# Differential attention: spread query split on GpSimd, query rows on ScalarE, earlier row transposes on TensorE

## The reference, cut to what matters

```
h  = layernorm(x)                          # rows of 256
q, k = rotary(h @ Wq, h @ Wk); v = h @ Wv  # 16 heads, 2 sets of probabilities
p_r = softmax(q_r k_r^T * scale + causal)  # r = 0, 1
a  = p_0 v - lambda * p_1 v                # per head, then RMS norm over its 16 values
x  = x + (a * gain * (1 - lambda_init)) @ Wo
```

## Time and profile before

| | |
|---|---|
| median of 3 runs | 1345.92 us (1343.61 to 1348.31) |
| the profiled execution | 1350.3 us, span 1348.3 us |
| mean granted TensorE clock | 0.964 |
| granted clock from 134.8 to 168.5 us (fifth of the page's 40 slices) | 0.7 of full speed |
| busy share of the span | PE 91%, DVE 71%, ACT 52%, POOL 34% |
| differential attention | from 0 to about 227 us of the span |

### The profile page before, as it was taken

One profiled execution on the slowest core, in us unless ns is written; L12 is line 12 of the kernel. 1 busy time (PEld: TensorE's weight loads), 2 busy tenths in 40 slices (PEclk: granted clock), 3 DMA queues, 4 the chain that ended last, 5 costly groups with the idle time before them and its releaser, 6 DMA issues. The chain is left out here.

```text
span 1348.3 us, 27677 instructions
## 1 busy us (share of the span) xinstructions
PE 1223.6 (91%) x9976; PEld 974.3 (72%) x9976; DVE 961.7 (71%) x1865; ACT 707.6 (52%) x1471; POOL 454.6 (34%) x537
## 2 busy tenths in 40 slices
PE   5998797889898788699799999999997899999998
PEld 3676565344444367698677887878787899999998
DVE  6888686788888375788477777878675658555555
ACT  3777473678787536200356566565653463333332
POOL 2443542255544314466443242323321211112210
PEclk8999799799999978899899999999999999999999
DMA  5111052033232030000400000000000300000001
GB/s 172 37 33 35 24 122 69 11 88 85 81 90 65 10 104 1 0 0 0 146 5 8 4 6 5 4 8 4 8 0 1 95 25 25 25 25 24 1 1 63
DMA packets 58657, 51.00 MB, mean 38 GB/s; under 512 B 9064, under 2 KB 50888, under 8 KB 58184
## 3 DMA queue, kind: packets, MB, share of 16 engines
q1 hardware_dynamic: 58574, 49.88, 13.2%
HBM read 37.93 MB, written 11.53 MB: 37 GB/s over the span
## 5 line engine op out<-in xcount | busy, mean ns | idle before, releaser
L839 DVE TENSOR_REDUCE fa_neg_max<-psum 128x2 f32<-128x512 f32 x256 | 163.5, 685 | 35.1 <-PE psum L1012 34.2
L898 ACT ACTIVATE fa_probs<-psum 128x1024 f32<-128x1024 f32 x128 | 130.4, 1020 | 45.6 <-PE psum L1017 44.7
L1869 PE MATMUL psum<-mo_xT_high,mo_w_high 128*128 128x256 f32 x512 | 144.5, 282 | 2.1 <-DVE mo_xT_low L2703 1.9
L1869 PE MATMUL psum<-mo_xT_low,mo_w_high 128*128 128x256 f32 x512 | 144.1, 282 | 0.0
L1869 PE MATMUL psum<-mo_xT_high,mo_w_low 128*128 128x256 f32 x512 | 143.5, 280 | 0.0
L2535 ACT ACTIVATE mo_silu<-psum 128x256 f32<-128x256 f32 x128 | 49.1, 385 | 154.7 <-PE psum L1869 154.7
L2669 DVE TENSOR_TENSOR mo_mid<-mo_silu,psum 128x256 f32<-128x256 f32 x128 | 53.6, 420 | 92.8 <-ACT mo_silu L2535 92.7
L1012 PE MATMUL psum<-stacks_k_stack,stacks_q_stack 48*128 48x256 bf16 x512 | 93.0, 286 | 17.0 <-DVE fa_neg_max L839 8.5
L2005 POOL TENSOR_TENSOR ga_probs<-ga_probs,ga_top 128x1024 f32<-128x1024 f32 x16 | 30.5, 1906 | 205.4 <-DVE ga_top L2159 205.4
L1869 PEld LDWEIGHTS psum<-mo_xT_high,mo_w_high 128*128 128x128 f32 x512 | 96.3, 188 | 2.5 <-DVE mo_xT_low L2703 2.1
L1869 PEld LDWEIGHTS psum<-mo_xT_low,mo_w_high 128*128 128x128 f32 x512 | 96.4, 188 | 0.0
(11 more groups left out here) (433 smaller groups left out, 3575.7 us busy)
## 6 DMA issues: line engine op xcount, KB each, us to landing
k_parts<-da_k_parts SPq DMA_DIRECT2D x96, 64.0 KB, 2.0
stacks_k_stack<-k_parts SPq DMA_DIRECT2D x32, 192.0 KB
q_parts<-stacks_parts SPq DMA_DIRECT2D x48, 64.0 KB, 2.0
stacks_q_stack<-q_parts SPq DMA_DIRECT2D x32, 96.0 KB
x<-in_x SPq DMA_DIRECT2D x4, 512.0 KB, 5.8
da_context<-in_ctx SPq DMA_DIRECT2D x4, 512.0 KB, 7.6
stacks_q_stack<-q_parts SPq DMA_DIRECT2D x32, 64.0 KB
fa_context<-in_ctx SPq DMA_DIRECT2D x16, 128.0 KB, 2.2
```

Source lines behind the costliest of these rows:

```text
L839: nc.vector.tensor_reduce(neg_max[:, b, :, head_at(h)], ps[:, h % 2, :].rearrange("p (q k) -> p q k", q=2), AX.X, ALU.max, negate=True).th ...
L898: nc.scalar.activation(probs[:, g].rearrange("p h k q -> p h (k q)"), ps[:, 2 + 2 * (g % 2):4 + 2 * (g % 2), :], ACT.Exp).then_inc(exp_don ...
L1869: done = nc.tensor.matmul(out, lhsT[i], rhs[j], start=start and k == 0, stop=stop and k == 2)
```

## The change

`NORM_TURN` becomes 5. The statistics of the four tiles are taken at the end of turn 5. ACT takes the reciprocal root at the start of turn 6, behind the squares. DVE scales it at the end of turn 6 and makes one more small array, `q_offset` = -mean x rstd. ACT then makes one tile of `q_rows` and its high part in each of turns 7 to 10, in front of the copies of the turned probabilities. POOL splits one tile of queries in each of turns 8 to 11, between the keys of tile t+2 and `split_keys`. On PE the turn of the normalised rows of tile t+3 stands directly behind turn_probs(1), in front of the heads. Turns 5 to 12 are all straight code; one loop, of turns 1 to 4, is left.

```diff
-        NORM_TURN = 6
+        NORM_TURN = 5
 (pipeline)
-            for t in range(NORM_TURN, NORM_TURN + 4):
-                turn(t, lambda k: True)
-            with eng.Fori(NORM_TURN + 4, last) as t:
+            for t in range(NORM_TURN, last):
                 turn(t, lambda k: True)
 (POOL; split_queries also waits for q_rows_ready n + 1)
+                for n in range(RING):
+                    if at(t, NORM_TURN + 3 + n):
+                        split_queries(n)
+                        pool.wait_ge(q_split, n + 1)
                 if valid(t + 1):
                     split_keys(t + 1)
-                for k in range(2):
-                    if at(t, NORM_TURN + 2 + k):
-                        split_queries(2 * k)
-                        split_queries(2 * k + 1)
-                        pool.wait_ge(q_split, 2 * k + 2)
 (ACT, behind the squares)
+                if at(t, NORM_TURN + 1):
+                    first_ln.on_scalar(act)
+                for n in range(RING):
+                    if at(t, NORM_TURN + 2 + n):
+                        if n == 0:
+                            act.wait_ge(first_offset, 1)
+                        place = dict(bias=q_offset[:, n:n + 1], scale=first_ln.rstd[:, n:n + 1])
+                        nc.scalar.activation(q_rows[:, n], core.x[:, n, :], ACT.Identity, **place).then_inc(q_rows_ready, 1)
+                        nc.scalar.activation(stacks.parts[:, n, 0], core.x[:, n, :], ACT.Identity, **place).then_inc(q_highs, 1)
 (ACT, end of the turn)
-                if at(t, NORM_TURN):
-                    first_ln.on_scalar(act)
-                if at(t, NORM_TURN + 1):
-                    for n in range(RING):
-                        act.wait_ge(q_rows_ready, n + 1)
-                        nc.scalar.copy(stacks.parts[:, n, 0], q_rows[:, n]).then_inc(q_highs, 1)
 (DVE, start of the turn)
-                if at(t, NORM_TURN + 1):
-                    (wait, scale of first_ln.rstd, wait)
-                    for n in range(RING):
-                        first_ln.normalise(q_rows[:, n], n).then_inc(q_rows_ready, 1)
 (DVE, end of the turn)
+                if at(t, NORM_TURN + 1):
+                    (wait, scale of first_ln.rstd, wait)
+                    nc.vector.scalar_tensor_tensor(q_offset[:], first_ln.mean[:], -1.0, first_ln.rstd[:], ALU.mult, ALU.mult).then_inc(first_offset, 1)
 (PE; the same block, with its waits for xn_ready, v_kept and shifted[0], moved from behind L671 to directly behind turn_probs(1))
+                if valid(t + 3):
+                    ...
+                    for c in range(KC):
+                        done = nc.tensor.transpose(ps[:, 3, c * P:(c + 1) * P], xn[:, c * P:(c + 1) * P], ident[:])
+                    done.then_inc(xT_psum, 1)
```

More of the change, by code:

```diff
@@ L252, in differential_attention @@
         k_parts, k_rest = sb("k_parts", [P, TILES, PARTS, E], BF16), sb("k_rest", [P, E])
+        q_offset = sb("q_offset", [P, RING])
         q_rows, q_rest = sb("q_rows", [P, RING, E]), sb("q_rest", [P, E])
@@ L272, in differential_attention @@
         rot_products, rot_swaps = sem("rot_products"), sem("rot_swaps")
+        first_offset = sem("first_offset")
         LOADS = 7 * 16
-        NORM_TURN = 6
+        NORM_TURN = 5
         block = scope.enter_context(nc.Block())
@@ L367, in split_queries @@
             def split_queries(n):
+                pool.wait_ge(q_rows_ready, n + 1)
                 pool.wait_ge(q_highs, n + 1)
@@ L528, in shift @@
                         top[:, r, :, None].to_broadcast([P, D_HEADS, SEQ]), ALU.min, ALU.subtract).then_inc(shifted[r], 1)
-                if at(t, NORM_TURN + 1):
-                    dve.wait_ge(first_ln.ready, 1)
-                    nc.vector.tensor_scalar(first_ln.rstd[:], first_ln.rstd[:], C_HD ** -0.5, None, ALU.mult).then_inc(first_scaled, 1)
-                    dve.wait_ge(first_scaled, 1)
-                    for n in range(RING):
-                        first_ln.normalise(q_rows[:, n], n).then_inc(q_rows_ready, 1)
                 if valid(t + 3) and not started(t, 1):
@@ L587, in turn @@
                     first_ln.on_vector(dve)
+                if at(t, NORM_TURN + 1):
+                    dve.wait_ge(first_ln.ready, 1)
+                    nc.vector.tensor_scalar(first_ln.rstd[:], first_ln.rstd[:], C_HD ** -0.5, None, ALU.mult).then_inc(first_scaled, 1)
+                    dve.wait_ge(first_scaled, 1)
+                    nc.vector.scalar_tensor_tensor(q_offset[:], first_ln.mean[:], -1.0, first_ln.rstd[:], ALU.mult, ALU.mult).then_inc(first_offset, 1)
                 if isinstance(t, int) and t < 0:
@@ L648, in turn @@
                     turn_probs(1)
+                if valid(t + 3):
+                    pe.wait_ge(xn_ready, t + 4)
+                    if valid(t + 2):
+                        pe.wait_ge(v_kept, t + 3)
+                    if valid(t + 1):
+                        pe.wait_ge(shifted[0], t + 2)
+                    for c in range(KC):
+                        done = nc.tensor.transpose(ps[:, 3, c * P:(c + 1) * P], xn[:, c * P:(c + 1) * P], ident[:])
+                    done.then_inc(xT_psum, 1)
+                if valid(t):
                     pe.wait_ge(values_ready, t + 1)
@@ L672, in turn @@
                     done.then_inc(attnT_psum, 1)
[L673 to L681, removed]
                 if valid(t):
```

## The result

The changed kernel takes **1331.6 us** (median of 4 runs, 1330.35 to 1332.79) against 1347.1 of before in the same session (1343.61 to 1348.87): ratio 0.988, interval 0.9854 to 0.9905, so 15.5 us faster. The forecast was 1328.2, from 1345.9 by 17.7.

A forecast was written before the change was run, and what follows sets the result against it. PE was busy for 91% of the span, with turns 7 to 10 16.8 us too long. Terms -16.8 + 0.4 + 0.6 - 1.6 - 0.3 = -17.7 us, from the median of 1345.92 to 1328.2; range 1323.8 to 1334.

The forecast's parts named there:

- rivals 1 and 2: Rival 1: transposes give nothing, 1329.8 us; rival 2: DVE bounds turns 8 to 11, 1329.8 us; together chance 0.17.
- The long turns: Turns 7 to 10, where query work sat in lumps, fall to 11.27 us each: -16.8 us.
- The cover on ACT and POOL: ACT's two activations in turns 7 to 10 and POOL's one-tile split in turns 8 to 11 stay hidden: 0.
- The second cover on POOL: Behind `split_keys`, from POOL's end of the values until PE takes them in turn 6: another 1.27 us.
- SP: Query parts complete in turn 11 instead of 10; 8 us of cover before the next sublayer's first load: 0.
- POOL against DVE: Splits in turns 8 to 11 lengthen DVE's combination of the heads: +0.4 us for four turns, bounds 0 and 2.0.
- Statistics: Turn 6's rotary products late behind DVE's chain, +0.5 us, and two small operations, +0.1; bounds 0.2 and 1.3 together.
- Transposes: PE's two transposes moved before the heads save 0.13 us in each of turns 1 to 12: -1.6 us.
- Straight code: Turns 5, 11 and 12 leave a loop, 0.11 us less each: -0.3 us, bounds +1 and -0.5.
- Rival 6: Later sublayers meet the falls of PE's clock otherwise, 3 us either way; beyond the other rivals, chance 0.07.

The follow-up runs named there:

- e3: The changed kernel again, with no edit: 1335.0 us, ratio 0.9902 to the kernel before.
- e1: The changed kernel with the two transposes of the normalised rows back in their old place, behind the turn of the scaled rows: 1335.9 us, ratio 0.9913 to before.
- e6: The kernel before with turns 6 to 12 as straight code, nothing else: 1343.9 us (one run).
- e4: The changed kernel with POOL's split of one query tile behind `split_keys` instead of in front of it: 1334.3 us, ratio 0.9917 to before.
- e7: The changed kernel with POOL's split of one tile a turn in front of the keys instead of behind them: 1332.9 us, ratio 0.9903 to before.
- e11: The changed kernel with the split in front of the keys and turns 1 to 12 all straight code, no loop: 1328.3 us, ratio 0.9867 to before.
- e9: The kernel before, query work untouched, with turns 5 to 12 as straight code: 1349.3 us, ratio 1.0014 to before.
- e10: The changed kernel with the split in front of the keys and straight code from turn 4: 1332.5 us, ratio 0.9897 to before.

## Why the prediction held, and where it did not

The forecast's change of 17.7 us was 15.5, and 11.7 in the second measurement (e3). Of the 3.4 us by which 1331.6 lies above 1328.2, 1.2 are the baseline (1347.1 for 1345.9) and 2.2 the change. So it lies just above the 1326 to 1331 that I gave my own sizes, where I had put rivals 1 and 2 (1329.8 to 1332.1), and neither of them came true. The range held it, but with room left for other things: the +2.5 us in the mixture stood at nothing. By terms:

- *The long turns.* Forecast -16.8; e1, the spread alone, shortens the stretch by 16.0 with 0.3 lost in turn 6 and 0.17 in each of turns 9 to 12. PE's granted clock is 1.00 from 30 us to 214 us now. The 0.7 that I read for turns 9 and 10 was the page's digit with the rest cut off; the view of that slice says 0.80. Without the transposes the terms add up to -16.1, which e1 meets with -16.0. Right, though the size before is itself not fixed: 163.8, 163.2 and 163.8 in three profiles of that code or nearly so, and 161.3 in e6, by how long PE's clock was low. The gain in the stretch is 17.4 to 18.1 us.
- *The cover on ACT and POOL.* Right: 0.47 and 0.35 us left. The second cover on POOL was mis-sized, 1.27 for 1.7 (e4).
- *SP.* Right: its last stores are issued by 203.5 us, and the next sublayer's first load starts at 212.4.
- *POOL against DVE.* Forecast +0.4, measured +0.25 (e7). The instruction named does take 0.89 instead of 0.48 us, but all of that is hidden; the cost comes by the bound's wait for POOL's first copy of the values. The rule of the Trainium skill, page "SBUF — State Buffer", section "Who interferes with whom", names the wait of the combination rightly, and the +1.3 to +1.4 us estimated by it did not come.
- *Statistics.* Forecast +0.6, measured +0.2 (turn 6 at 11.33 against 11.14) and nothing for the two small operations. The maxima of turn 6 are 0.33 us late, but so late that the bound misses POOL's copy: 0.17 us where straight turns have 0.31, which gives 0.14 back. I also took the last small operation's end, 108.38 in the earlier trace rows, for the start of the next; in the trace after it begins before that one ends, as the rows below show.
- *Transposes.* Forecast -1.6, measured -2.1 (e1): 0.11 a turn in turns 1 to 5, 0.22 from turn 6 on, where DVE's scaled rows are late.
- *Straight code.* Forecast -0.3, three turns; the 0.13 us a turn are there in e11, and mostly gone where the transposes stand in their old place (e6). But the term had a second part that I left out: **+2.5 us in the mixture**, by a load of instructions beside its first weights (e9, e10, e11). This is the step that was missing. Stretch and mixture together, -18.1 + 2.5 = -15.6, come near the 15.5 us of the medians; medians that vary by 3.4 us for the changed kernel alone cannot confirm it to a tenth. In the profiled execution the part between gave another 4.9, which hid it. That is chance: this part took 845.96 and 841.90 us in two profiles of before, 841.05 and 842.29 in two of changed.
- *Elsewhere.* Rival 6 gave 3 us either way, for the clock in later sublayers; the part between differs by 4.1 us in the two profiles of before. The lead, up to the scores of turn 1, varies by 3 us besides, which no rival named.

```profile
98.80 0.59 DVE L108 SCALAR_TENSOR_TENSOR first_var<-first_spread,first_half 128x4 f32<-128x4 f32 x1
99.31 0.54 DVE L541 TENSOR_TENSOR da_rot_b<-psum,da_rotary 128x384 f32<-128x384 f32 x1
100.24 1.21 DVE L519 TENSOR_REDUCE da_top<-psum 128x16 f32<-128x1024 f32 x1
```

## What to carry to other kernels

Put side work into the idle time that stands in front of a wait for another engine, not behind the work which that engine waits for: two tiles at once cost 5.8 to 6 us a turn in the one place and at most 0.55 in the other. Fill a stand of PE with work that must be done anyway, even if only part of it comes through. When POOL's work moves, look at the short DVE operations in the middle of dependent chains, not only at the long ones: a bound of 0.17 us that became 0.31 made whole turns longer, a combination that took 0.4 us more did not. After adding or removing straight code, look at the starts of all later stages: a stage that begins with a load on the critical path is worth a look at the DMA view for instruction loads.

## What the runs showed of the hardware

In the seven profiles with a load of 16,384 bytes of instructions that starts 1.0 to 2.4 us into the mixture, that sublayer's first weights reach ACT 1.2 to 1.9 us later than in the six without. PE then stands 2.7 to 3.4 us instead of 1.5 to 2.0, and in each of the seven, and in none of the six, its clock is granted at the lower level, 1.2 GHz, soon after; the mixture takes 301.6 to 303.6 us instead of 298.8 to 299.3. SP shows the load too: in each of the seven, and in none of the six, one of its DMA issues takes 1.0 to 2.1 us instead of 0.43 to 0.47. After, then before:

```profile
1030.46 1.16 SPq L2451 DMA_DIRECT2D mo_w_route<-in_mo_w_route  x1
...
1050.53 0.47 SPq L2448 DMA_DIRECT2D mo_w_route<-in_mo_w_route  x1
```

The first weights were issued before that, so SP's late issue is not what delays them. No run moved the load alone: that it delays the weights is argued from these thirteen profiles, in which load and delay always come together. The Trainium skill, page "Runtime: NRT & Kernel Launch", section "Instruction fetch mechanics", says that each sequencer brings its instructions in blocks of 16 KiB by a DMA queue of its own and that this is mostly hidden; the size agrees (other instruction loads here have 8,192 bytes, on a second queue), and here it is not hidden. Which engine's load it is stays open; shifting one engine's code alone would tell.

A DVE operation on 128x16 numbers (the bound, 0.17 us alone) that starts inside a POOL instruction and would end before it ends 0.03 us behind it instead: 0.30 to 0.44 us long in 83 cases over 13 traces. The three that started less than 0.01 us behind POOL's took their 0.17 us.

How long PE's clock stays low behind the same stand differs from one execution to the next (3.4 or 6.8 us behind the splits of before). So a stand costs more than its length, and by a varying amount.
